# Transposed keys in two stacked orders: one made by the engines, the other copied by DMA

## What is computed

```python
x = x + _layernorm(_L0_attn_ref(_layernorm(x), ...))    # 4 heads of 64
x = x + _layernorm(_L0_ffn_ref(_layernorm(x), ...))     # 8 experts, argmax of a gate

# inside _L0_attn_ref
xn = _layernorm(x, ln_gamma, ln_beta)
q, k, v = proj(w_q), proj(w_k), proj(w_v)               # [b, 4, 2048, 64]
qn = _rmsnorm(q, q_gamma) * dh ** (-0.5)
kn = _rmsnorm(k, k_gamma)
sim = jnp.einsum('bhid,bhjd->bhij', qn, kn)
out = jnp.einsum('bhij,bhjd->bhid', jax.nn.softmax(sim, axis=-1), v)
```

## Time and profile before

| what | value |
|---|---|
| median of 3 runs | 746.66 us (744.32 to 750.18) |
| profiled execution, span | 747.7 us |
| preparation, batch 0, after its first weights | 22.6 to 94.6 us |
| attention, batch 0 | 94.6 to 304 us |
| preparation, batch 1 | 339 to 412 us |
| attention, batch 1 | 412 to 611 us |
| experts and what stands before them | 611 to 747.7 us |
| PE's mean granted clock | 0.939 |

### The profile page before, as it was taken

The page is one execution under the profiler, slowest core; times in us unless marked ns, Lnnn a source line. Parts: engine busy times, 40 slices in busy tenths (PEclk is TensorE's granted clock), DMA queues, the critical chain, the costliest instruction groups (busy, mean ns, idle before and its releaser), DMA issues.

```text
span 747.7 us, 21776 instructions
## 1 busy us (share of the span) xinstructions
PE 620.8 (83%) x8758; PEld 431.1 (58%) x8774; DVE 597.9 (80%) x1145; ACT 546.2 (73%) x878; POOL 291.2 (39%) x457
## 2 busy tenths in 40 slices
PE   4788879999989999857878799999999996277571
PEld 2566636666655666745666366666666675147470
DVE  4998869998889889897898688798888879736462
ACT  3488988888878888764789888788888876325551
POOL 2233435455635543003566332333323211516463
PEclk9899999999999999977999999999999999679885
DMA  5920058988878988121011588889898850244431
GB/s 175 267 74 2 0 100 150 169 166 162 162 140 144 176 157 157 57 82 47 25 34 37 106 160 153 156 149 165 150 164 146 154 128 10 81 139 130 131 100 37
DMA packets 56313, 88.69 MB, mean 119 GB/s; under 512 B 6801, under 2 KB 25492, under 8 KB 56214
## 3 DMA queue, kind: packets, MB, share of 16 engines
q0 software_dynamic: 35088, 66.13, 46.2%
q1 hardware_dynamic: 20550, 21.17, 10.0%
q10 hardware_dynamic: 576, 0.00, 0.0%
HBM read 15.87 MB, written 14.66 MB: 41 GB/s over the span
## 4 chain that ended last, share of the span: by engine, by line
PE 46%; DVE 24%; ACT 10%; DMA 9%; issue 8%; another core or an unknown queue 1%; POOL 0%; SPq 0%; POOLq 0%; DVEq 0%; ACTq 0%
PE banks L1382 15%; PE banks L1232 7%; PE banks L1400 6%; PE banks L1401 6%; PE banks L1402 5%; DVE e_l L998 5%; DMA e_h<-e_f 4%; DMA e_x<-x_all 4%; PE banks L1284 3%; ACT e_f L607 2%; DVE x_all L1055 2%; DVE e_h L842 1%; DVE ss L853 1%; DVE st L1068 1%
## 5 line engine op out<-in xcount | busy, mean ns | idle before, releaser
L998 DVE TENSOR_TENSOR e_l<-e_f,e_h 128x1024 f16<-128x1024 f32 x172 | 212.8, 1263 | 32.5 <-DMA e_h<-e_f 30.5
L607 ACT ACTIVATE e_f<-banks,nbias,c_ 128x1024 f32<-128x1024 f32 x172 | 199.5, 1201 | 42.4 <-PE banks L1382 41.7
L1382 PE MATMUL banks<-q_T,k_T 128*128 128x512 f16 (+1 forms) x1024 | 205.8, 386 | 4.7 <-DVE e_l L872 3.4
L1402 PE MATMUL banks<-v_mm,e_l 128*128 128x65 f16 x2048 | 202.1, 191 | 0.0
L1402 PEld LDWEIGHTS banks<-v_mm,e_l 128*128 128x128 f16 x2048 | 189.8, 99 | 0.0
L1400 PEld LDWEIGHTS banks<-v_mm,e_h 128*128 128x128 f16 x1376 | 126.2, 96 | 42.3 <-DVE e_l L998 21.7
L1400 PE MATMUL banks<-v_mm,e_h 128*128 128x65 f16 x1376 | 137.0, 193 | 7.0 <-DVE attn_x L1010 4.9
L451 POOL DMA_DIRECT2D e_h<-e_f x148 | 79.3, 536 | 154.4 <-ACT e_f L607 144.3
L1401 PE MATMUL banks<-v_mm,e_h 128*128 128x64 f16 x1376 | 136.5, 195 | 0.0
L1401 PEld LDWEIGHTS banks<-v_mm,e_h 128*128 128x128 f16 x1376 | 127.4, 97 | 0.1
L998 DVE TENSOR_TENSOR e_l<-x_all,e_x 128x1024 f16<-128x1024 f32 x84 | 105.9, 1282 | 19.2 <-DMA e_x<-x_all 16.6
(11 more groups left out here) (272 smaller groups left out, 1212.7 us busy)
## 6 DMA issues: line engine op xcount, KB each, us to landing
e_h<-e_f POOLq DMA_DIRECT2D x148, 256.0 KB, 3.8
e_x<-x_all POOLq DMA_DIRECT2D x72, 256.0 KB, 3.9
x_all<-x SPq DMA_DIRECT2D x12, 512.0 KB, 3.8
rows_d<-e_x SPq DMA_DIRECT2D x1, 5180.0 KB, 25.4
k_T<-rows_d SPq DMA_DIRECT2D x20, 259.0 KB, 4.0
x_all<-weT SPq DMA_DIRECT2D x2, 512.0 KB, 10.9
x_all<-weT SPq DMA_DIRECT2D x4, 256.0 KB, 4.3
x_all<-x SPq DMA_DIRECT2D x8, 128.0 KB, 3.5
```

The lines of the kernel that those rows point to most:

```text
L607: act.activation(whole[s % ALL % NEF], ps_S[s % ALL % 3], ACT.Exp, bias=bias_of(h, k // NT), scale=CESC).then_inc(s_E, 1)
L998: dve.tensor_tensor(low[s % ALL % NLO], whole[s % ALL % NEF], high[s % ALL % NHI], ALU.subtract).then_inc(s_El, 1)
L1382: ins = pe.matmul(ps_S[s % ALL % 3][:, c * BANK:(c + 1) * BANK], k_T[rows, 1 - c if cross else c, h * N + j * P:h * N + (j + 1) * P], q_T[ ...
L1402: ins = pe.matmul(o, low[s % ALL % NLO][:, at], v[:, 0:DH + 1], start=False, stop=j == NT - 1, skip_group_check=True)
```

## The change

The tile buffer `qk_s` holds two columns for each head, 128 wide: [high, low], or [low, high] in the tiles of groups 1 and 3 (`swapped`). `high_qk` is one ACT instruction in place of two, `low_qk` writes the same number of elements at another place, and counts of the semaphore `s_hi` are halved. PE transposes 4 key blocks in place of 8, and `move_k` moves 512 columns in place of 1024, into the stack that `swapped` names. When `s_ke` says that a group's four tiles have been moved, SP issues two DMAs that copy the group's keys into the other stack, with partitions 0 to 63 and 64 to 127 exchanged: 64 partitions by 4 heads by 512 f16 each, 256 KB each, in pieces of 1 KB. The first `scores` that read a group (head 0, query block 0, key tiles 0, 4, 8, 12) wait for a new semaphore `s_kc`. `turned_keys(0)` stands in SP's list ahead of the loads of the later experts' weights, `turned_keys(1)` ahead of batch 1's last reloads.

```diff
--- before.py
+++ after.py
@@ -81,7 +81,7 @@
         qk_n = [e_l16[:, i * 4 * D:(i + 1) * 4 * D].bitcast(f32) for i in range(2)]
         e_h16 = e_h[:, :, :].rearrange("p s n -> p (s n)")
         xhat = e_h16[:, 0:2 * TG * D].bitcast(f32).rearrange("p (t d) -> p t d", d=D)
-        qk_s = [a[:, 2048:2048 + 6 * H * DH].rearrange("p (h c) -> p h c", h=2 * H)
+        qk_s = [a[:, 2048:2048 + 4 * H * DH].rearrange("p (h c) -> p h c", h=2 * H)
                 for a in (e_h16, e_l16)]
         q_sq = e_h16[:, 3584:3584 + 2 * D].bitcast(f32)
 
@@ -176,7 +176,7 @@
         ps_V = [bank(4)[:, 0:D], bank(5)[:, 0:D]]
         ps_VG = [bank(4)[:, 0:DG], bank(5)[:, 0:DG]]
         ps_TQ = bank(6).bitcast(f16)[:, 0:H * P]
-        ps_TK = bank(7).bitcast(f16)[:, 0:2 * H * P]
+        ps_TK = bank(7).bitcast(f16)[:, 0:H * P]
         ps_Y = [[bank(2 + i % 2 * 2 + t)[:, 0:DG] for t in range(2)] for i in range(NP)]
         ps_R = bank(6)[:, D:D + (MT + 1) * NE].rearrange("p (t e) -> p t e", e=NE)
         ps_TX = [bank(i).rearrange("p (k t c) -> p k t c", k=KH, t=2) for i in range(2)]
@@ -212,6 +212,7 @@
         s_o = [sem(f"s_o{i}") for i in range(NOT)]
         s_wx = [sem(f"s_wx{i}") for i in range(NE // 2)]
         s_cast = [sem(f"s_cast{i}") for i in range(NHI)]
+        s_kc = [sem(f"s_kc{i}") for i in range(NG)]
 
         s_id, s_ones, s_wf, s_qg, s_q2 = sems("id ones wf qg q2")
 
@@ -259,6 +260,9 @@
 
         def swapped(at):
             return at * P // BANK % 2
+
+        def keys(a, rows, gi):
+            return k_T[rows, a, :].rearrange("p (h n) -> p h n", h=H)[:, :, gi * TG * P:(gi + 1) * TG * P]
 
         def groups(body):
             for gi in range(NG):
@@ -308,6 +312,14 @@
             sp.wait_ge(s_xh, KH * WSLOTS)
             for k in range(KH):
                 sp.dma_start(raw_we[:, k], weT_k[:, k, 0:WSLOTS]).then_inc(s_we, 16)
+            def turned_keys(b):
+                for gi in range(NG):
+                    a = swapped(gi * TG)
+                    sp.wait_ge(s_ke, b * NT + (gi + 1) * TG)
+                    sp.dma_start(keys(1 - a, slice(0, DH), gi), keys(a, slice(DH, P), gi)).then_inc(s_kc[gi], 16)
+                    sp.dma_start(keys(1 - a, slice(DH, P), gi), keys(a, slice(0, DH), gi)).then_inc(s_kc[gi], 16)
+
+            turned_keys(0)
             for e in range(WSLOTS, NE):
                 sp.wait_ge(s_wl2, KH * (e - WSLOTS + 1))
                 sp.dma_start(raw_we[:, :, e - WSLOTS, :], weT_k[:, :, e]).then_inc(s_wx[e - WSLOTS], 16)
@@ -318,6 +330,8 @@
                     sp.dma_start(x_all[:, at, :], x_d[:, at, :]).then_inc(s_xw, 16)
 
             for b in range(0, NB):
+                if b:
+                    turned_keys(b)
                 for i in range(NEF - 4):
                     at = XT + i * TG
                     sp.wait_ge(s_El, max(s for s in range((b + 1) * ALL) if s % ALL % NEF == 4 + i) + 1)
@@ -545,8 +559,8 @@
                     act.wait_ge(s_qg, n + 1)
                     if n - 1 > 0:
                         act.wait_ge(s_T2, n - 1)
-                    for first, at in ((0, 2 * DH), (H, 0)) if swapped(n % NT) else ((0, 0), (H, 2 * DH)):
-                        act.activation(qs[:, first:, at:at + DH], qn[:, first * DH:].rearrange("p (h d) -> p h d", d=DH), ACT.Copy).then_inc(s_hi, 1)
+                    hi = DH * swapped(n % NT)
+                    act.activation(qs[:, :, hi:hi + DH], qn.rearrange("p (h d) -> p h d", d=DH), ACT.Copy).then_inc(s_hi, 1)
 
                 def move_q(n, at):
                     if n == 0:
@@ -557,8 +571,8 @@
 
                 def move_k(n, at):
                     act.wait_ge(s_T2, n + 1)
-                    act.activation(k_T[:, :, :].rearrange("p a (h n) -> p h a n", h=H)[:, :, :, at * P:(at + 1) * P],
-                                   ps_TK.rearrange("p (h a n) -> p h a n", h=H, a=2), ACT.Copy).then_inc(s_ke, 1)
+                    act.activation(k_T[:, swapped(at), :].rearrange("p (h n) -> p h n", h=H)[:, :, at * P:(at + 1) * P],
+                                   ps_TK.rearrange("p (h n) -> p h n", h=H), ACT.Copy).then_inc(s_ke, 1)
 
                 def root_of_largest():
                     act.wait_ge(s_mxB, b * NQB + 1)
@@ -865,8 +879,8 @@
                     dve.wait_ge(s_dq, 2 * n + 2)
                     if n - 1 > 0:
                         dve.wait_ge(s_lo, n - 1)
-                    if 2 * n - 2 > 0:
-                        dve.wait_ge(s_hi, 2 * n - 2)
+                    if n - 1 > 0:
+                        dve.wait_ge(s_hi, n - 1)
                     if n - 1 > 0:
                         dve.wait_ge(s_q2, n - 1)
                     dve.tensor_tensor(qk_n[t % 2].rearrange("p (h d) -> p h d", d=DH),
@@ -874,10 +888,11 @@
                                       spread(rn[:, :], 2, DH), ALU.mult).then_inc(s_qkn, 1)
 
                 def low_qk(n, at, t):
-                    dve.wait_ge(s_hi, 2 * n + 2)
+                    dve.wait_ge(s_hi, n + 1)
                     qs = qk_s[t % 2]
-                    hi = 2 * DH * swapped(at)
-                    dve.tensor_tensor(qs[:, :, DH:2 * DH], qk_n[t % 2].rearrange("p (h d) -> p h d", d=DH),
+                    hi = DH * swapped(at)
+                    lo = DH - hi
+                    dve.tensor_tensor(qs[:, :, lo:lo + DH], qk_n[t % 2].rearrange("p (h d) -> p h d", d=DH),
                                       qs[:, :, hi:hi + DH], ALU.subtract).then_inc(s_lo, 1)
                     dve.wait_ge(s_q2, n + 1)
                     dve.tensor_reduce(qn2[:, at:at + 1, :].rearrange("p o h -> p (o h)"),
@@ -986,7 +1001,7 @@
                     s = hh * STEPS + k
                     if s < b * ALL + 2:
                         dve.wait_ge(s_q2, end - 1 + k)
-                        dve.wait_ge(s_hi, 2 * (end - 1 + k))
+                        dve.wait_ge(s_hi, end - 1 + k)
                     if s == b * ALL + 2:
                         dve.wait_ge(s_T2, end)
                     if s - NLO + 1 > 0:
@@ -1299,12 +1314,9 @@
                 if n > 0:
                     pe.wait_ge(s_ke, n)
                 for h in range(H):
-                    at = DH * swapped(n % NT)
-                    pe.transpose(ps_TQ[:, h * P:(h + 1) * P], qs[:, h, at:at + 2 * DH], ident16[:, :])
+                    pe.transpose(ps_TQ[:, h * P:(h + 1) * P], qs[:, h, :], ident16[:, :])
                 for h in range(H):
-                    for a in range(2):
-                        ins = pe.transpose(ps_TK[:, (2 * h + a) * P:(2 * h + a + 1) * P],
-                                           qs[:, H + h, a * DH:(a + 2) * DH], ident16[:, :])
+                    ins = pe.transpose(ps_TK[:, h * P:(h + 1) * P], qs[:, H + h, :], ident16[:, :])
                 ins.then_inc(s_T2, 1)
 
             for b in range(0, NB):
@@ -1376,6 +1388,8 @@
                             if cross:
                                 if s - 2 > 0:
                                     pe.wait_ge(s_E, s - 2)
+                                if h == 0 and qb == 0 and j % TG == 0:
+                                    pe.wait_ge(s_kc[j // TG], (b + 1) * 32)
                             for c in range(QB // BANK):
                                 rows = slice(0, P) if cross else slice(c * DH, (c + 1) * DH)
                                 at = h * N + qb * QB + c * BANK
```

## The result

| | before | after |
|---|---|---|
| median | 747.56 us (744.32 to 753.98, 20 runs) | 744.01 us (739.56 to 750.72, 20 runs) |
| ratio | | 0.9956 (95% interval 0.9938 to 0.9974) |
| profiled execution, span | 747.7 us | 746.9 us |

What follows compares the result with a forecast made beforehand. DVE was taken to bound the preparation and ACT's list the attention's start. Gains of 4.6 us in preparation and 2.8 at the attention, less 1.0 for copies, gave 6.4 us: 740.3 us, range 735.0 to 745.5.

Steps and rivals of the forecast that it cites:

- The head of the attention with its copies: Steps 0 to 12: 0.97 us a batch gained behind the table load, 0.5 us a batch lost to copies delaying casts.
- the 1.6 us of waits for the squares: Preparation: four of DVE's nine waits for ACT's squares (L527) shrink, 0.78 + 0.42 + 0.44 = 1.6 us.
- ACT's prices: ACT's list in each tile: the second `high_qk` copy saves 0.33 us, the halved `move_k` 0.42 us.
- the waits for the root: Preparation: DVE's eleven waits for ACT's root of the norms (L541); nine fall by 0.33 us each, 3.0 us.
- The one that I called fixed: Eleventh wait for the root, in a stretch begun by the end of `low_y`, without copy or transposes: no gain.
- the wait at 353 us: Batch 1: a DVE wait for the squares of 1.2 us loses 0.42 us through four fewer transposes.
- those of the last groups: Last group of each batch: a 0.7 us wait for the squares behind full-clock transposes loses 0.22 us each.
- The five behind `low_y`: Five of nine waits for the squares, at the end of the fixed stretch from `low_y`: 1.4 us that stay.
- The 0.78 us of group 2: Batch 0, group 2: a wait for the squares behind late ACT moves and transposes at 1.2 GHz goes entirely, 0.78 us.
- nothing at DVE: Rival, chance 0.13: ACT's savings become another wait of DVE; only the attention's head gains, 1.8 us, 744.9 us.
- slower by the clock: Rival, chance 0.05: less-busy PE drops to 1.2 GHz, about 1.2 us a tile; with 14 more such tiles 757.1 us.
- collision: Rival, chance 0.14: copies push back the casts of steps 1 to 4 by their full length; 3.6 us gained, 743.0 us.

Runs made afterwards that it cites:

- transposes_back: The changed kernel with the four removed key transposes of each tile put back, their results unread: 743.72 us, ratio 0.9921 to the kernel before.
- the two kernels with one stack: The changed kernel without copies, scores reading one stack, partition halves kept apart (output wrong): ratio 0.9894 to the kernel before; with 20 idle PE matmuls added, 0.9907.
- one_stack_b: The changed kernel without copies or their waits, scores reading one stack, partition halves kept apart (output wrong): 740.47 us, ratio 0.9894 to the kernel before.
- halves: The changed kernel with group 3's copies split, tiles 12 and 13 copied as soon as moved, 14 and 15 later: 744.58 us, ratio 0.9947.
- early_copy: The changed kernel with group 3's copies issued with group 2's, taking group 2's keys again (wrong data, same bytes): 725.21 us, ratio 0.9944 to the kernel before.
- copies_twice: The changed kernel with group 3's two copies made a second time once the first have landed: 746.84 us, ratio 0.9981 to the kernel before.
- the fillers: Idle PE matmuls, 20 ahead of the transposes of tiles 3 and 7: changed kernel ratios 0.9887 and 0.9916, kernel before 0.9977; 24 at more places, changed kernel 0.9934.

## Why the prediction was half right

Two terms of the sum failed. The head of the attention with its copies, 0.9 us less in the forecast, became 1.1 us more: the copies and the casts overlap at a price that I had put at 0.5 us a batch, and it is about 1.2. And the 1.6 us of waits for the squares came only in part, because one of them was no property of the kernel and because PE lost clock, a cost that the forecast did not hold.

**Right: ACT's prices.** 0.33 and 0.42 us for a tile were forecast, 0.30 and 0.42 measured.

**Right: the waits for the root.** Nine of eleven were to go, 3.0 us; all eleven went, 3.9 us. The one that I called fixed went as a wait and gave nothing, as the forecast had it: its stretch from `low_y` to the sums at its end takes 4.69 us (38.99 to 43.68, and 39.31 to 44.00), and what DVE no longer waits for the root it waits for the squares. Before and after:

```profile
38.99 1.21 DVE L849 TENSOR_TENSOR n_l<-banks,n_h 128x1024 fp32r<-128x1024 f32 x1
...
41.42 0.17 DVE L861 SCALAR_TENSOR_TENSOR nm<-nr,rcol 128x8 f32<-128x8 f32 x1 [0.23 <-ACT nr L541]
...
43.68 0.69 DVE L853 TENSOR_REDUCE ss<-e_f 128x8 f32<-128x512 f32 x1 [0.20 <-ACT e_f L527]
```

```profile
39.31 1.21 DVE L863 TENSOR_TENSOR n_l<-banks,n_h 128x1024 fp32r<-128x1024 f32 x1
...
44.00 0.69 DVE L867 TENSOR_REDUCE ss<-e_f 128x8 f32<-128x512 f32 x1 [0.53 <-ACT e_f L541]
```

**Right in part, wrong as a sum: the waits for the squares.** They were to fall by 1.6 us and rose by 0.3 in the trace. One by one: the wait at 353 us was to lose 0.42 us and went from 1.22 to 0.79, those of the last groups were to lose 0.22 each and went from 0.74 to 0.55. The five behind `low_y` grew from 1.4 to 2.4 us in stretches of fixed length, which costs no time but hides the gain in this view. The 0.78 us of group 2 went to 0.38, and 0.6 us of new waits stand in groups that have 3.4 us at 1.2 GHz. Three things were missed.

- 0.78 us of it was no property of the kernel. It stood in one row beside a granted clock of 0.91, and a second execution does not have it. I had one trace and built a term on its only disturbed stretch outside the first groups.
- A DVE that no longer waits for the root comes earlier to the next tile's sums, and the squares that these need hang on PE's projection. `transposes_back` shows this: 2.5 of 3.9 us come back. The rival "nothing at DVE" named the mechanism and priced it as all or nothing.
- PE lost clock. Averaged over the timed executions of a set, the granted clock was 0.942, 0.944 and 0.945 for the kernel before and 0.937, 0.936 and 0.934 for the changed one (on the third chip it was 0.956 for the kernel before). With the removed transposes put back it is 0.944. A difference of 0.008 is 12 us more at 1.2 GHz. A group with about 3.5 such us took 17.66 instead of 17.21, so 0.13 us for each; if the 12 us cost as much wherever they lie, that is some 1.6 us in all, an estimate that no run tests, since most of the low clock lies outside the preparation. The rival "slower by the clock" was real; its price of 1.2 us a tile was far too high, since most of a projection at 1.2 GHz hides behind DVE. The Trainium skill, "TensorE: Matmul & The Clock Gate", Part 1, ties the clock to how busy PE was just before; the traces agree in part (the row at 48.48 stands behind 2.11 us of idle time, but the row at 48.39, behind the same stand, is followed by full clock). The price here is set by what hides the slow matmuls.

**Right at full clock: the groups.** Groups 1 and 2 were to take about 17.2 us each and in batch 0 take 17.21 or 17.22 where the clock stays at 1.00; in batch 1, where both took 17.8 to 17.9 us before, they take 17.6 and, for the low clock, 17.8 to 18.0. The last group was to lose 0.42 + 0.22 us and what its waits gave, and fell from 15.77 to 14.5 us in both batches.

**Right in kind, wrong in size: the head and its price.** From step 0 to step 2 the forecast was 0.97 us less in each batch. The kernel before takes 5.3 and 5.4 us there, the changed one 4.3 at full clock and 4.7 to 4.9 where PE is at 1.2 GHz: 0.5 to 1.0 less. The copies were put at 0.5 us a batch with bounds of 0 and 1.9. Step 0 to 12 takes 19.9 us without copies (four stages of the two kernels with one stack, 19.5 to 20.1) and 21.1 with them: 1.2 us a batch. So a stretch that should have become 0.5 us shorter became 0.5 longer. What would show this was named: a new wait of DVE for a cast. It is there, in DVE's order of time in the second execution of the changed kernel and, behind it, in `one_stack_b`:

```profile
105.33 1.23 DVE L1013 TENSOR_TENSOR e_l<-e_f,e_h 128x1024 f16<-128x1024 f32 x1 [3.07 <-DMA e_h<-e_f]
```

```profile
103.00 1.23 DVE L1010 TENSOR_TENSOR e_l<-e_f,e_h 128x1024 f16<-128x1024 f32 x1 [0.83 <-DMA e_h<-e_f]
```

The two issue this cast, the third, within 0.1 us of each other; with the copies (issued at 98.31 and 98.94 us) it lands 5.3 us after its issue, without them 3.1. POOL's order of time, with and without:

```profile
99.91 0.53 POOL L465 DMA_DIRECT2D e_h<-e_f  x1 [1.91 <-ACT e_f L621]
```

```profile
99.82 0.53 POOL L462 DMA_DIRECT2D e_h<-e_f  x1 [1.90 <-ACT e_f L618]
```

The third execution has 5.9 us and a wait of 3.61, the first 3.8 us and 0.70: what the copies cost depends on how they fall against the casts.

Why the free engine time did not hide it shows in the stretches: in the earlier trace rows the engines were at 0.36 from 102 to 104 us, and I subtracted all the free time there. But steps that start earlier bring their casts earlier too, into the same hole (the third cast is issued at 102.35 us before and at 100.31 in the first execution of the changed kernel):

```profile
102.00:104.00 2.00, 1.32 (x38) 1.23 (x39) 1.50 (x2) 1.79 (x2) 0.99 (x2) 1.00 1.09 206
104.00:106.00 2.00, 2.00 (x25) 0.84 (x22) 1.71 (x3) 0.29 (x1) 0.54 (x1) 1.00 1.07 189
```

The share is 1.09 from 102 to 104 us. The gain and the copies wanted the same idle time, and I gave it to one of them. The 1.2 us is the least certain figure here: a second pair of copies cost 0.5 us a batch, copies moved away gave 0.8, and the kernel before with copies lost 0.6. The rule of the Trainium skill on one set of 16 DMA engines ("DMA: Bandwidth & Descriptors", "Issuing engines are not separate DMA queues") pointed the right way: the price it led to, 1.9 us a batch, and my 0.5 lie on either side of 1.2. That the rival "collision", 3.6 us gained, lies so near to the measured 3.5 is luck: it had the whole 4.6 us of the preparation and too high a price for the copies.

**The ledger.** Microseconds, both batches together; measured are means over two traces of the kernel before and six (preparation) or three (steps 0 to 12) of kernels whose stage is that of the changed kernel (the three executions of the changed kernel itself, `halves`, `early_copy` and `copies_twice`).

| stage | forecast | measured |
|---|---|---|
| up to step 0 (batch 0: from the start; batch 1: from step 127 of batch 0) | -5.4 | -3.3 |
| steps 0 to 12 | -0.9 | +1.1 |
| sum | -6.3 | -2.2 |
| medians | -6.4 | -3.0 to -4.0 |

The stages leave about 1 us less gain than the medians do. By the three executions of the changed kernel alone the first row is -4.2 and the sum -3.1, and nothing is left over; with only two traces of the kernel before, the rows are no surer than that. Should there be a rest, it lies in the attention behind step 12 or in the last stage, and those vary by 3 to 6 us from execution to execution, so no trace can place it.

**What stays open.** How much of the gain of the fillers is clock. In the traces they give 0 to 0.9 us in the groups of batch 0 and 0.3 to 0.5 in those of batch 1, but step 0 comes no earlier (93.3 to 93.8 us in the kernels with fillers in groups 1 and 2, 92.9 to 94.1 without them), while the medians fall by 1 to 5 us. Part of that lies in steps 0 to 12 (20.3 us on average with the 20 fillers, 21.1 without), and why fillers long before should help there no run tells. Something like it holds for `transposes_back`: its preparations are only 1.4 us shorter than before's in all (step 0 at 95.0 us), its steps 0 to 12 took 20.2 us on average, and its median is as good as the changed kernel's. It may be how the steps fall against the casts; that is argued, not shown.

## What to carry to other kernels

A wait that you shorten on one engine's list is worth only what the next wait behind it does not take back: follow the waiting engine to its next releaser, and ask who releases that one. Idle time of a shared resource beside your change can be spent once; if the change also brings the other users forward, count them there first. And a term that rests on one stretch with a lower clock than its neighbours needs a second execution before it goes into a sum; so does the account of what went wrong, for the changed kernel's first trace had such stretches too.

## What the runs showed of the hardware

- Two 64-row matmuls on different halves of the partitions overlap and on the same half don't: the eight score matmuls of two steps took 1.50 against 1.92 us, and the kernel 5.3% longer than the one before.
- Removing work from a PE that was not the bound lowered its granted clock over the whole kernel, from 0.944 to 0.936 on average; the same work put back, for nobody, gave 0.944 again. A group with 3.4 us at 1.2 GHz took 0.45 us longer.
- Two copies of 256 KB issued just ahead of a cast delayed its landing from 3.1 to 5.3 us.
- The four sets differ in one stage: the part behind the attention took 120 us on one chip and 135 to 142 on the others, with the preparation and the attention alike to about 1% on average. Why, no run tells.
